# First layer: the chosen experts alone, in 39 tiles of sorted rows laid into the scan's chunks

## What is computed

```python
x = L0_attn_x
xn = _layernorm(x, axis=-1)
x = x + _L0_attn_ref(xn, ...) + _L0_ffn_ref(xn, ...)
```

```python
router_logits = x @ w_gate
probs = jax.nn.softmax(router_logits, axis=-1)
topk_w, topk_ids = jax.lax.top_k(probs, TOPK)
topk_w = topk_w / jnp.sum(topk_w, axis=-1, keepdims=True)
gu = jnp.einsum('th,ehf->etf', x, w_gate_up)
act = _silu_and_mul(gu)
eo = jnp.einsum('eti,eih->eth', act, w_down)
routed = jnp.einsum('te,eth->th', combine, eo)
shared = _silu_and_mul(x @ w_sh_gate_up) @ w_sh_down
```

## Time and profile before

| | us |
|---|---|
| median of 3 runs | 1718.62 (1711.59 to 1721.74) |
| the profiled execution | 1723.52, span 1721.8 |
| PE busy in the span | 1423.6 (83%) |
| DVE busy | 926.6 (54%) |
| ACT busy | 538.0 (31%) |
| POOL busy | 350.5 (20%) |
| mean granted TensorE clock | 0.914 |

### The profile page before, as it was taken

One profiled execution on the slowest core, in us unless ns is written; L12 is line 12 of the kernel. 1 busy time (PEld: TensorE's weight loads), 2 busy tenths in 40 slices (PEclk: granted clock), 3 DMA queues, 4 the chain that ended last, 5 costly groups with the idle time before them and its releaser, 6 DMA issues. The chain is left out here.

```text
span 1721.8 us, 22117 instructions
## 1 busy us (share of the span) xinstructions
PE 1423.6 (83%) x7388; PEld 861.4 (50%) x7388; DVE 926.6 (54%) x1942; ACT 538.0 (31%) x825; POOL 350.5 (20%) x311
## 2 busy tenths in 40 slices
PE   5987798769876987799999989888935398988986
PEld 2445445554444445556666654444533255644464
DVE  6366444735474537451320348898878444657434
ACT  1454054504451446122222223223301132233321
POOL 2145004600271027220030011000012600000034
PEclk9998799969997899899999989899965699999998
DMA  6110001100110013030000036000000200111113
GB/s 230 28 50 26 2 16 55 32 2 1 47 56 2 1 28 124 1 100 0 1 0 0 0 126 213 0 0 1 1 1 20 91 26 19 32 37 49 59 48 109
DMA packets 62074, 70.35 MB, mean 41 GB/s; under 512 B 16839, under 2 KB 48007, under 8 KB 61834
## 3 DMA queue, kind: packets, MB, share of 16 engines
q1 hardware_dynamic: 58892, 60.55, 11.2%
q0 software_dynamic: 3072, 8.39, 1.5%
HBM read 51.83 MB, written 17.08 MB: 40 GB/s over the span
## 5 line engine op out<-in xcount | busy, mean ns | idle before, releaser
L315 PE MATMUL l_b<-l_xnT,all_region_a 128*128 128x512 f32 x544 | 255.2, 620 | 15.9 <-ACTq L558 13.0
L315 PEld LDWEIGHTS l_b<-l_xnT,all_region_a 128*128 128x128 f32 x544 | 106.0, 199 | 143.2 <-issue 113.4
L666 POOL TENSOR_TENSOR all_region_b<-all_region_b,l_lc 128x512 f32<-128x512 f32 x64 | 93.2, 1472 | 326.0 <-DMA all_region_b<-l_lc_rows 325.7
L315 PE MATMUL l_b<-all_region_a,l_hT 128*128 128x256 f32 x384 | 114.1, 423 | 0.0
L1458 PE MATMUL l_banks<-l_xnT,mid_region_c 128*128 128x512 f32 (+1 forms) x192 | 96.1, 654 | 16.9 <-DVE l_xnT L1642 16.9
L855 DVE TENSOR_TENSOR l_hT<-all_region_b,l_b 128x512 f32<-128x512 f32 x48 | 33.0, 687 | 139.5 <-PE l_b L315 117.1
L2306 POOL TENSOR_TENSOR l_rstd<-l_moments,all_neg_half 128x4 f32<-128x4 f32 x20 | 20.8, 1038 | 337.6 <-DVE l_moments L2347 337.6
L315 PEld LDWEIGHTS l_b<-all_region_a,l_hT 128*128 128x128 f32 x384 | 72.7, 204 | 24.5 <-issue 15.3
L678 POOL TENSOR_TENSOR l_rw<-l_xdt,l_decay 128x512 f32<-128x512 f32 x64 | 72.6, 1165 | 35.3 <-DVE l_xdt L834 35.3
L315 PE MATMUL l_b<-all_region_b,l_xp 128*32 128x32 f32 x2048 | 31.6, 205 | 52.5 <-DVE all_region_b L871 52.5
L581 ACT ACTIVATE all_region_b<-all_region_b 128x512 f32<-128x512 f32 x64 | 69.4, 1084 | 17.9 <-PE l_b L315 14.3
(11 more groups left out here) (393 smaller groups left out, 2763.7 us busy)
## 6 DMA issues: line engine op xcount, KB each, us to landing
all_region_b<-l_lc_rows SPq DMA_DIRECT2D x256, 64.0 KB, 2.0
l_slots_in<-mid_zeros SPq DMA_DIRECT2D x1, 4992.0 KB, 22.8
mid_vector_rows<-l_slots_in SPq DMA_DIRECT2D x39, 128.0 KB, 2.1
l_slots_out<-all_region_a SPq DMA_DIRECT2D x39, 128.0 KB, 1.7
all_region_a<-l_gate_up SPq DMA_DIRECT2D x1, 4096.0 KB, 14.8
all_x<-x SPq DMA_DIRECT2D x4, 512.0 KB, 5.4
all_region_a<-w_gate_up SPq DMA_DIRECT2D x1, 2048.0 KB, 17.5
all_region_a<-l_down SPq DMA_DIRECT2D x1, 2048.0 KB, 19.1
```

Of the source, the lines that this page charges most:

```text
L315: return nc.tensor.matmul(out, lhsT, rhs, start=start, stop=stop, **kw)
L666: nc.gpsimd.tensor_tensor(bc[:, k, :, :], bc[:, k, :, :], spread(lc[:, c, heads], 1, BLK), ALU.subtract).then_inc(dd_ready.sem, 1)
```

## The change

- The hardware loops of layer 0 are written out. All 2048 tokens are normalised and routed in group 0's front: PE turns the rows of groups 1 to 3 between the projection blocks of group 0 ("early"), DVE ranks all logits at once (`route`), then computes all step sizes and the slots (`dispatch`), and only then the convolutions of group 0.
- POOL scatters the normalised rows (32 indirect DMAs of 128 rows: 16 ahead of group 0's first differences, 8 behind its first weighing, 8 behind its first gate) into a table that SP has cleared with five DMAs.
- The units in the front are the four shared ones; six of their eight down jobs are in the front, two in chunk 0.
- 39 tiles with an expert each go through a pipeline of **steps**. At one place, PE has the gate-up product of tile f-1, the transpose of the hidden rows of f-2, the down product of f-3 and the two transposes of the rows of f; ACT a tanh, a copy out and a copy of the turned rows; DVE two products and a copy. silu(g) is written as 0.5 g (1 + tanh(g/2)). The 42 steps lie in the 40 places of ten chunks: chunks 2 and 3 of group 0 and all of groups 1 and 2, two places with two.
- POOL fetches the results from group 3 on, and DVE adds them between that group's convolutions and at the ends of its chunks, two tiles after the last output add.
- The next group's rows are normalised in chunk 2 and turned in chunk 3 of the group before; the block sums stand ahead of the projections.
- A chunk's decay rows for one piece are one DMA where they were four. Layer 3 shares the table and its semaphores with layer 0, and the table is no longer cleared between them.

```diff
@@ -174,47 +168,109 @@
...
+    STEPS = MOE_TILES + 3
+    places = [(g, c, k) for g in range(GROUPS - 1) for c in range(NCH) for k in range(PIECES) if (g, c) >= (0, 2)]
+    places = sorted(places + [places[-1], places[-3]])
+    assert len(places) == STEPS
+    steps_at = {}
+    for f, place in enumerate(places):
+        steps_at.setdefault(place, []).append(f)
+
+    def tile_jobs(f):
+        back = (("gu", f - 1), ("th", f - 2), ("dn", f - 3), ("tx", f))
+        return [(job, i) for job, i in back if 0 <= i < MOE_TILES]
...
@@ -274,335 +312,476 @@
...
+        def tile_step(f):
+
+            if 0 <= f - 1 < MOE_TILES:
+                i = f - 1
+                if i == 0:
+                    pe.wait_ge(w.moe_sem, 32)
+                n = expert[i] = pe.value_load(owner[0:1, i:i + 1], min_val=0, max_val=N_EXP - 1)
+                jobs.wait_room(pe, 0, ("gu", i))
+                pe.wait_ge(xgT_ready.sem, xgT_ready.done(0, i))
+                for k in range(DK):
+                    part = w.gate_up[:, bass.ds(n * DK + k, 1), :]
+                    last = mm(jobs.bank(("gu", i))[:, 0:2 * P], xgT[i % 2][:, k, :], part.rearrange("p a n -> p (a n)"),
+                              k == 0, k == DK - 1)
+                jobs.fill(last, ("gu", i))
+            if 0 <= f - 2 < MOE_TILES:
+                i = f - 2
+                pe.wait_ge(h_ready.sem, h_ready.done(0, i))
+                jobs.wait_room(pe, 0, ("th", i))
+                jobs.fill(nc.tensor.transpose(jobs.bank(("th", i))[:, 0:P], hm[i % 2], ident[:, :]), ("th", i))
+            if 0 <= f - 3 < MOE_TILES:
+                i = f - 3
+                jobs.wait_room(pe, 0, ("dn", i))
+                pe.wait_ge(hT_ready.sem, hT_ready.done(0, i))
+                part = w.down[:, bass.ds(expert[i] + SHARED, 1), :]
+                jobs.fill(mm(jobs.bank(("dn", i))[:, 0:DIM], hmT[i % 2], part.rearrange("p a n -> p (a n)")), ("dn", i))
+            if f < MOE_TILES:
+                pe.wait_ge(moe.xg_landed[f % 3], 16 * (f // 3 + 1))
+                jobs.wait_room(pe, 0, ("tx", f))
+                for k in range(DK):
+                    last = nc.tensor.transpose(jobs.bank(("tx", f))[:, k * P:(k + 1) * P],
+                                               xg[f % 3][:, k * P:(k + 1) * P], ident[:, :])
+                jobs.fill(last, ("tx", f))
+
...
-        with pe.Fori(0, BATCH) as b:
-            with pe.Fori(0, HALVES) as half:
-                g = b * HALVES + half
-
...
+        pe.wait_ge(xa_ready.sem, xa_ready.done(0, 0))
+        turn_rows("xT", 0, xa)
+        pe.wait_ge(w.in_sem, 16)
+        side(0, xnT)
+        blocks = ((0, 1, 2), (3, 4, 5), (6, 7, 8))
+        for g in range(1, GROUPS):
+            for j in blocks[g - 1]:
+                in_proj(0, j)
+            pe.wait_ge(xa_ready.sem, xa_ready.done(0, g))
+            turn_rows("early", g, xa[:, g * GT:(g + 1) * GT, :])
+            side(g, xnT2)
+        in_proj(0, CONV_BLK + Z_BLK - 1)
+        pe.wait_ge(ranked.sem, 1)
+        jobs.wait_room(pe, 0, "counts")
+        every = chosen[:, :, :].rearrange("p t e -> p (t e)")
+        mm(jobs.bank("counts")[:, 0:P], prior, every)
+        jobs.fill(mm(jobs.bank("counts")[:, P:2 * P], ones[:, 0:P], every), "counts")
+        pe.wait_ge(a_ready.sem, 1)
+        for g in range(GROUPS):
+            sums(g)
+            if g > 0:
+                pe.wait_ge(xnT_dve.sem, xnT_dve.done(0, GROUPS - 1 + g))
+                pe.wait_ge(xnT_act.sem, xnT_act.done(0, GROUPS - 1 + g))
                 for j in range(CONV_BLK + Z_BLK):
-                    c0 = HID + j * P if j < CONV_BLK else (j - CONV_BLK) * P
-                    bk, at, use = in_slot(j)
...
-                for c in range(NCH):
-                    from_before(c)
-                    for k in range(PIECES):
-                        near(c, k)
-                        down(g, EARLY + c * PIECES + k)
-                        if k == 1 and c + 1 < NCH:
-                            by_tokens(c + 1)
-                        if k == 2 and c + 1 < NCH:
-                            b_and_cb(c + 1)
-                        if k == 3 and c > 0:
-                            out_proj(g, c - 1)
-                    assemble(c)
-                out_proj(g, NCH - 1)
+            pe.wait_ge(w.ffn_sem, 16 * 2)
+            for u in range(SHARED):
+                if u == SHARED - 1:
+                    pe.wait_ge(xbc_ready.sem, xbc_ready.done(g))
+                    by_tokens(g, 0)
+                    b_and_cb(g, 0)
+                unit(g, u)
+                if u > 0:
+                    down(g, 2 * u - 2)
+                    down(g, 2 * u - 1)
+            for c in range(NCH):
+                from_before(g, c)
+                for k in range(PIECES):
+                    near(g, c, k)
+                    if k == 1 and c + 1 < NCH:
+                        by_tokens(g, c + 1)
+                    for f in steps_at.get((g, c, k), []):
+                        tile_step(f)
+                    if c == 0 and k % 2 == 1:
+                        down(g, 2 * SHARED - 2 + k // 2)
+                    if k == 2 and c + 1 < NCH:
+                        b_and_cb(g, c + 1)
+                    if k == 3 and c > 0:
+                        out_proj(g, c - 1)
+                    if (c, k) == (NCH - 1, 1) and g + 1 < GROUPS:
+                        pe.wait_ge(xn_ready.sem, xn_ready.done(0, g))
+                        turn_rows("xT", g + 1, xn)
+                assemble(g, c)
+            out_proj(g, NCH - 1)
...
@@ -649,92 +838,117 @@
...
+        def scatter(t):
+
+            if t == 0:
+                pool.wait_ge(moe.slots_ready, 1)
+                pool.wait_ge(cleared, 16 * CLEARS)
+            for i in range(TOP_K):
+                nc.gpsimd.indirect_dma_start(slots_in, bass.IndirectOffsetOnAxis(slot_u[:, i, t:t + 1], 0),
+                                             xa[:, t, :], None).then_inc(moe.scattered, 16)
+
...
+        for g in range(GROUPS):
+            if g == GROUPS - 1:
+                for t in range(2 * GT):
+                    fetch(t)
+            if g == 0:
+                for t in range(2 * GT):
+                    scatter(t)
+            differences(g, 0)
+            weigh(g, 0)
+            if g == 0:
+                for t in range(2 * GT, 3 * GT):
+                    scatter(t)
+            for c in range(NCH):
+                if c + 1 < NCH:
+                    differences(g, c + 1)
+                    weigh(g, c + 1)
+                if c > 0:
+                    out_scale(g, c - 1)
+                gate(g, c)
+                if (g, c) == (0, 0):
+                    for t in range(3 * GT, 4 * GT):
+                        scatter(t)
+                if g == GROUPS - 1:
+                    for t in range(2 * GT + 2 * c, 2 * GT + 2 * c + 2):
+                        fetch(t)
+            out_scale(g, NCH - 1)
...
@@ -744,196 +958,346 @@
...
+        def tile_step(f):
+
+            if 0 <= f - 1 < MOE_TILES:
+                i = f - 1
+                dve.wait_ge(s_ready.sem, s_ready.done(0, i))
+                if i >= 2:
+                    jobs.wait_filled(dve, 0, ("th", i - 2))
+                bank = jobs.bank(("gu", i))
+                nc.vector.scalar_tensor_tensor(out=hm[i % 2], in0=tanh[:, i % 2, :], scalar=1.0, in1=bank[:, 0:P],
+                                               op0=ALU.add, op1=ALU.mult)
+                dve.drain()
+                nc.vector.scalar_tensor_tensor(out=hm[i % 2], in0=hm[i % 2], scalar=0.5, in1=bank[:, P:2 * P],
+                                               op0=ALU.mult, op1=ALU.mult).then_inc(h_ready.sem, 1)
+                jobs.free(dve.drain(), ("gu", i))
+            if 0 <= f - 2 < MOE_TILES:
+                i = f - 2
+                jobs.wait_filled(dve, 0, ("th", i))
+                if i >= 2:
+                    jobs.wait_filled(dve, 0, ("dn", i - 2))
+                nc.vector.tensor_copy(hmT[i % 2], jobs.bank(("th", i))[:, 0:P]).then_inc(hT_ready.sem, 1)
+                jobs.free(dve.drain(), ("th", i))
+
...
         dve.wait_ge(mem.const_ready, mem.n_const)
         dve.wait_ge(mask_ready.sem, 1)
+        route()
         for q in range(NB):
             rows = slice(q * BLK, (q + 1) * BLK)
             nc.vector.tensor_copy(diag[rows, :], before[rows, 0, rows])
             nc.vector.tensor_copy(turn[:, q, :].rearrange("p (s e) -> p s e", s=4),
                                   ident[:, :].rearrange("p (s r e) -> p s r e", s=4, r=NB)[:, :, q, :])
+        step_sizes()
+        dispatch()
         dve.wait_ge(mem.col_ready, 16)
...
+        for g in range(GROUPS):
+            for j in range(CONV_BLK):
+                conv(g, j)
+                if g == GROUPS - 1:
+                    add(j)
+            for u in range(SHARED):
+                hidden(g, u)
+                if u > 0:
+                    down_add(g, 2 * u - 2)
+                    down_add(g, 2 * u - 1)
```

(52 more changed lines are left out.)

1256 lines of the change are left out of this document (699 added, 557 removed).

## The result

| | before | after |
|---|---|---|
| median of 4 runs, us | 1718.96 (1711.59 to 1721.74) | 1661.82 (1660.01 to 1666.60) |
| ratio | | 0.9683, 95% interval 0.9655 to 0.9712 |
| span of the profiled execution, us | 1721.8 | 1664.9 |
| end of the first layer, us | 730.5 | 672.2 |

57 us faster, where 119 were forecast; the time lies 7 us above the range. All of the difference is in the first layer: behind it the span is 991.3 us before and 992.7 after. The profiled execution of the changed kernel was the slowest of its four, 4.8 us above their median, so a difference against its trace can be some us too large.

The account below looks back on a forecast made before the run. It took PE to bound the first layer's fronts and a loop through all engines its chunks. Terms -96.8 - 40.7 + 0 + 4.5 + 15 - 5 + 3.7 = -119 us gave 1600 us, range 1560 to 1655.

Parts of the forecast that it names:

- Steps in ten chunks: First layer's ten chunks carrying tile steps: the 42 steps in 40 places lengthen each chunk by 1.5 us, +15 us.
- every step waits once for each engine: Upper bound for a step chunk: waits at the places where nothing else is queued, +6 us a chunk.
- The transitions: Last assembly to next near product, groups 1 and 2: 103.8 us becomes 55.4, gain 48.4 twice, -96.8 us.
- the 6.4 of the sum: Transition's last work: place 2.55, relu to end of exp 3.0 and DVE's near product 0.9, 6.4 us.
- six convolutions at 3.24 us: Transition term in the fronts: DVE's convolutions set the pace at 3.24 us each, 19.4 us.
- Group 3: Last group: six fetched tiles added between convolutions cost 7.7 us, path gains 40.7; its chunks, losing down jobs, gain about 5.
- Group 0: First group's front, routing all 2048 tokens: near begins at 111 us, no gain or loss, bounds -8 to +10.
- late scatters: POOL's 16 later scatters in group 0's chunks 0 and 1: differences pushed back up to 9 us, eating missing downs' savings.
- The register read: PE's read of the expert's number in each step: at most 13 us, mostly covered and inside the steps' charge.
- The chunks stretch: Rival, 25%: ACT's step waits for PE and delays next-chunk exps that DVE's near needs; +5.5 a chunk, 1640 us.
- everything a little faster: Rival, 16%: hardware loops go, steps cost nothing, and eight chunks gain 1.5 us by cheaper waits and clock; 1573 us.
- End to end: Rival, 3%: DVE always late, so each step's engine work runs in a row, 5.4 us for 1.05; 1768 us.

Follow-up runs that it names:

- e4: Changed kernel with all 39 tiles left out (loads, products, stores) and the fetch and sum of the experts' rows in the first layer: 1586.04 us, ratio 0.9228.
- e2: Changed kernel with the new tile's turn put first in each step instead of last, on PE and ACT; same work: 1647.72 us, ratio 0.9579.
- e6: Changed kernel with POOL's subtractions for groups 1 to 3 held back until DVE's last convolution: 1653.10 us, ratio 0.9599.
- e15: Changed kernel plus two POOL waits for DVE near products, in group 3's and group 0's chunks; same work and order: 1658.69 us, ratio 0.9638.
- e10: Changed kernel without POOL's 16 late scatters, so the last two groups' rows never reach the experts' slots: 1655.27 us, ratio 0.9602.
- e1: Changed kernel with each tile's expert number a constant, so PE reads no register before gate-ups: 1670.70 us, ratio 0.9723.
- e16: e12 plus the state's product ahead of a group's first near product and e15's two POOL waits: 1625.28 us, ratio 0.9445.
- e12: Changed kernel with new tile turned first, expert numbers read in the fronts, and POOL's subtractions held behind the convolutions: 1632.10 us, ratio 0.9472.

## Why the prediction was wrong

The first layer between milestones of PE's timeline, in us. "Chunks" as above, "transition" from there to the next near product:

| stage | before | on record | after | e4, no tiles |
|---|---|---|---|---|
| to the first near product | 110.6 | 111 | 114.0 | 111.9 |
| chunks, group 0 | 74.4 | 78.9 | 87.7 | 75.0 |
| transition | 103.8 | 55.4 | 63.2 | 60.0 |
| chunks, group 1 | 74.4 | 81.9 | 95.0 | 69.8 |
| transition | 105.9 | 57.5 | 63.3 | 61.2 |
| chunks, group 2 | 74.2 | 81.7 | 93.8 | 71.1 |
| transition to group 3, with six adds | 103.7 | 63.0 | 68.7 | 61.7 |
| chunks, group 3 | 74.3 | 69.3 | 74.7 | 67.8 |
| to the layer's end | 9.3 | 13.0 | 11.7 | 10.1 |
| sum | 730.5 | 611.7 | 672.2 | 588.5 |

The miss of 60.5 us is 34 in the chunks of groups 0 to 2, 19 in the three transitions, 5 in group 3's chunks and 2 in the rest.

- **Steps in ten chunks, on record 15 us: 61.** This is the step that failed. I charged a step by the work that lies on DVE's path, 1.5 us a chunk, and took the stages of a tile to lie a place apart. They do not: DVE's products follow the gate-up of the same place, and the next turn waits for them through its PSUM bank. I wrote "every step waits once for each engine" as the upper bound, +6 a chunk; it was 6.1. With that bound alone the forecast would have been 1645, inside the range; the transitions took the time out of it. The order of jobs over three banks could have been counted from the code. e2 shows the part of the order, 20 us of the 61. What makes up the other 41 is argued, not shown. They go with work: in e2 the chunks of groups 1 and 2 take 15 to 17 us more than without tiles, and PE is busy some 20 us more (in group 1 74.4 for 54.1, though at a higher granted clock, 0.98 for 0.78). I had put only the last PE step on the path.
- **Chunks without tiles.** With the steps priced apart they took 75.0, 69.8 and 71.1 us for 75.9, 75.9 and 75.7 on record: the missing down jobs were worth 12 us more than I let them be. Without this the miss would be 72.
- **The transitions, gain 48.4 on record: 40.6 and 42.6.** The order of the path was right, with PE idle ahead of the hidden product (3.11 us); ACT's place to DVE's near product took the 6.4 of the sum. The path measured 63.2 and 63.3 us for 55.4. Mis-sized was first the term of six convolutions at 3.24 us: 22.5 us and 22.7 instead of 19.4, since POOL's subtractions now fall beside them; I took DVE's duration from a row where POOL rested. The stretch ahead of them took 17.0 and 15.8 us for 14.6, the stretch behind them 23.7 and 24.9 for 21.4. Behind them I had left out that PE's first near product stands behind its far product, which waits (4.41 us, for L1132) until DVE has read a bank, and DVE does that only behind its own near product: 2.4 us more. e6 gives back 6.2 and 4.8, the convolutions and some of the clock.
- **Group 3.** Adds between convolutions: 7.0 us by e4 for 7.7, right (part of it may be the 2 to 3 us by which e4's other transitions are shorter too). By its own terms the sum for group 3's chunks is -6, not -5. Its chunks were to gain 5 and gained nothing, by the one stall (e15: 67.7 us without it).
- **Group 0.** Near at 114.0 for 111, within its bounds. The late scatters cost 7.5 (e10), up to 9 on record, and as foreseen the missing downs paid for them: 75.0 without steps for 75.9.
- **The register read**, at most 13 us and mostly covered: the trace shows 0.1 to 0.8 us ahead of 29 of the 39 gate-ups, mostly 0.6, yet e1 gains nothing. That it was covered I had right, but not all of the cover: it is ACT's exps and DVE's queue. The Trainium skill's duration ("DMA: Bandwidth & Descriptors", Latency and other measured facts), some 600 ns a read, agrees with the trace; the estimate of 23 us on the path that was worked out from it does not.
- **The rivals.** "The chunks stretch" (25%, 1640) came nearest. ACT's queue is in it, but not as written: ACT was busy 15.9 us of the 23.8 of chunk 1 in groups 1 and 2 (21.6 of 29.6 in group 1's chunk 0), and DVE waited for tanh, not for exps. Of "everything a little faster" (16%, 1573) the first half fails, steps that cost nothing; what the end of the hardware loops is worth no run tests. "End to end" (3%) described the same loop with the whole of the price. The two should have been one rival, with a place's loop costed from rows. With near product 0.5, read 0.6, gate-up 1.0, tanh 0.3, DVE's two products 0.7, turn 0.4 and some hand-overs that is about 4 us, my estimate now; inside the chunks of group 1 the near products start 3.8 to 5.0 us apart.

## What to carry over

When work is dealt into places of an existing loop, list for each stage what it waits for in the same place, PSUM banks included: a rotation with as many jobs a step as banks plus one makes the last job wait for the first. Price it by the chain, not by the busiest engine. And before taking out a wait that a trace shows, ask what else runs beside it: of branches of one length, shortening a single one gives nothing, and which job comes first can be worth more than any of them.

## What was not expected of the hardware

- A DVE product of two SBUF tiles (128x512, else 0.63 to 1.8 us) stood 5.02 to 9.95 us in 26 places of 13 of the 15 kernels profiled after the one before (first layer; none in the kernel before, in e15 or in e16). Each ended 0.55 us after the end of a POOL product or subtraction of 128x512, at the end of a gapless run of such instructions; behind it POOL rested, issued a DMA, or had a product of 128x1. DVE's add of a fetched tile (128x256, else 0.49) stood 5.02 to 5.33 us at 15 more places, one of them in e15, and ended 0.29 us after such an end. The wait put into POOL took 7.7 us off a chunk in e15, and 8.8 in e16 (against e12).
- The granted clock moved with the work and its gaps. Without the reads (e1) it was 0.87 in a chunk for 1.00, and eight passes of the output projection took 3.76 us for 1.97. Without the tiles (e4) it was 0.78 in the chunks for 0.95, and so a kernel with less to do ran them on a slower PE.
